# Adding the input on GpSimd instead of VectorE, with the start and the edges put in another order, in a modulated convolution kernel

## What is computed

```python
def _layer(x, style, w, b, mw, mb, typ):
    s = style @ mw.T + mb
    weight = SCALE * w * s[:, None, :, None]
    demod = lax.rsqrt(jnp.sum(weight * weight, axis=(2, 3)) + EPS)
    weight = weight * demod[:, :, None, None]
    if typ == 'same':       # convolution + bias
    elif typ == 'upsample': # transposed convolution of stride 2 + bias, then blur (1,3,3,1)
    elif typ == 'downsample': # blur (1,3,3,1), then convolution of stride 2 + bias
for i, typ in enumerate(('same', 'upsample', 'same', 'downsample')):
    out = _layer(out, style, weights[i], biases[i], mod_w[i], mod_b[i], typ)
x = x + out
```

## Time and profile before

| | |
|---|---|
| median of 3 runs | 175.73 us (174.91 to 176.23) |
| profiled execution | 177.4 us, span 175.6 us |
| TensorE busy | 162.1 us, 92% of the span, 4015 records |
| VectorE busy | 136.0 us, 77% |
| GpSimd busy | 84.0 us, 48% |
| ScalarE busy | 56.0 us, 32% |
| mean granted clock of TensorE | 0.987 |
| transfers | 17.81 MB, mean 101 GB/s |

### The profile page before, as it was taken

How to read it: one execution, slowest core, us unless ns; L and a number is a source line. 1 busy time by engine, 2 the same in 40 slices (tenths; PEclk the granted TensorE clock), 3 DMA queues, 4 the chain that set the end, 5 groups by cost and what they waited for, 6 DMA issues and landing times. The chain is left out here.

```text
span 175.6 us, 8950 instructions
## 1 busy us (share of the span) xinstructions
PE 162.1 (92%) x4015; PEld 147.4 (84%) x4015; DVE 136.0 (77%) x239; ACT 56.0 (32%) x126; POOL 84.0 (48%) x138
## 2 busy tenths in 40 slices
PE   7999879979998899999899999999999999999960
PEld 5688766969767589899798999989899999999940
DVE  7639972789599598979496878787879797979992
ACT  3244533405113133333323233424242424231110
POOL 7009905218064081939173646464647473748400
PEclk9999978999999999999999999999999999999998
DMA  4970000030300301249082633333333343030332
GB/s 127 344 116 0 6 0 4 4 119 7 119 4 6 119 6 30 97 192 292 5 279 89 235 127 123 123 123 123 123 123 123 123 123 123 4 122 5 122 127 120
DMA packets 9382, 17.81 MB, mean 101 GB/s; under 512 B 4704, under 2 KB 5248, under 8 KB 9344
## 3 DMA queue, kind: packets, MB, share of 16 engines
q1 hardware_dynamic: 9280, 17.22, 28.7%
q10 hardware_dynamic: 64, 0.02, 0.1%
HBM read 8.85 MB, written 8.39 MB: 98 GB/s over the span
## 5 line engine op out<-in xcount | busy, mean ns | idle before, releaser
L187 POOL TENSOR_TENSOR Hw<-Hw 128x192 f32<-128x192 f32 x15 | 9.0, 600 | 67.3 <-DVE Hw L791 67.3
L458 PE MATMUL p_m<-uu,Hw 64*64 64x128 f32 x992 | 31.7, 268 | 0.0
L378 PE MATMUL p_lo<-xin,w0s 64*64 64x259 f32 x384 | 28.3, 407 | 1.9 <-DVE e_sb L817 1.9
L458 PEld LDWEIGHTS p_m<-uu,Hw 64*64 64x64 f32 x992 | 29.6, 132 | 0.0
L423 PE MATMUL p_le<-R_sb,F_st 64*64 64x128 f32 (+2 forms) x768 | 27.2, 275 | 1.2 <-issue 1.1
L378 PE MATMUL p_le<-xin,w0s 64*64 64x260 f32 x384 | 26.9, 391 | 0.0
L423 PEld LDWEIGHTS p_le<-R_sb,F_st 64*64 64x64 f32 x768 | 24.5, 139 | 1.9 <-issue 1.9
L448 PE MATMUL p_m<-u,Hw 64*64 64x256 f32 x384 | 25.8, 375 | 0.0
L802 DVE TENSOR_TENSOR uu<-u 128x516 f32<-128x516 f32 x32 | 23.8, 792 | 1.5
L654 ACT ACTIVATE u<-p_lo 128x518 f32<-128x518 f32 x16 | 9.7, 604 | 45.6 <-PE p_lo L378 45.6
L254 POOL COPY Hw<-Hw 64x896 f32<-64x896 f32 x15 | 23.6, 1575 | 0.9
(11 more groups left out here) (133 smaller groups left out, 216.5 us busy)
## 6 DMA issues: line engine op xcount, KB each, us to landing
xin<-in_x_dram SPq DMA_DIRECT2D x16, 512.0 KB, 4.3
out_dram<-ot SPq DMA_DIRECT2D x16, 512.0 KB, 3.1
wn<-in_L_cond_weights_dram SPq DMA_DIRECT2D x1, 192.0 KB, 3.3
mwn<-in_L_cond_mod_w_dram SPq DMA_DIRECT2D x1, 128.0 KB, 2.2
xe<-in_x_dram SPq DMA_DIRECT2D x2, 56.0 KB, 8.6
cn<-in_cond_dram ACTq DMA_DIRECT2D x1, 16.0 KB, 2.0
bn<-in_L_cond_mod_b_dram ACTq DMA_DIRECT2D x1, 1.0 KB
bn<-in_L_cond_biases_dram ACTq DMA_DIRECT2D x1, 1.0 KB
```

The lines of the kernel that those rows point to most:

```text
L378: ins = pe.matmul(bank[h * C:(h + 1) * C, s, 0:n], w0s[p % 2][rows, k, :], xin[p % NX][rows, i0:i0 + 2 * n - 1:2], start=(k == 0), stop=(k ...
L458: ins = pe.matmul(bank(h)[s * C:(s + 1) * C], tap(p, h, s, blk), moving(slice(h * C, (h + 1) * C), s, k), start=(k == 0), stop=(k == len(b ...
```

## The change

The changed kernel differs in these parts.

- VectorE's finish no longer writes z_sb. GpSimd adds x to s_sb and to e_sb (add_x, tiles sx), and finish writes the output tile ot straight from PSUM: the product times W_D3 plus sx, one STT for the odd and one for the even positions. For this the last demodulation has moved into s and e: t_sb is scaled by W_D3 on ScalarE, s_sb and e_sb are made in two halves each, as STT. VectorE waits for x_added_odd and x_added_even, GpSimd for s_made, e_made and z_made; put_edges(p) now waits for the finish of its pair.
- The weights are loaded twice, side by side (wn2), mod_w and wsum are copied twice, and one matmul with 128 columns stands for each two of 64 in the products of the start (`taps`, `both`). The transposes of wsum stand ahead of the style; V_st is copied by GpSimd.
- layer0_odd(1), layer0_even(1) and edge_x0 have moved from the loop into the start. In the loop edge_y, edge_z and edge_out stand at the end of TensorE's iterations 0, 1 and 2, and behind finish on VectorE.
- Loads wait for mid_done, and the three early stores have their own places in iterations 4, 6 and 8, behind m2_done.

```diff
+        wn2 = sb("wn", [C, LAYERS, 2, C, K])
+        wn = wn2[:, :, 0]
...
-        z_sb = bufs(sb, "z_sb", 2, [P, 2, 2 * NM])
-        e_sb = sb("e_sb", [P, 2, NM])
+        e_sb = bufs(sb, "e_sb", 2, [P, 2, NM])
+        sx = bufs(sb, "sx", 2, [P, 2, 2, NM])
...
+            pool.wait_ge(made["wsum"], 1)
+            pool.wait_ge(zeroed, 7)
+            V = wn[:, 2].rearrange("o i k -> o k i")
+            pool.tensor_copy(V_st[0:C], V).then_inc(copied["V_st"], 1)
+            pool.wait_ge(copied["V_st"], 1)
+            pool.tensor_copy(V_st[C:P], V).then_inc(copied["V_st"], 1)
...
             def put_edges(p):
+                pool.wait_ge(z_made, 2 * (p + 1))
...
+            def add_x(p, parity, to, signal):
+                x0 = xin[p % NX][:, 1 + EDGE + parity:1 + EDGE + parity + 1]
+                x0 = bass.AP(x0.tensor, x0.offset, [list(x0.ap[0]), [BASE, 2], [2, NM]])
+                pool.tensor_tensor(sx[p % 2][:, parity], to[:], x0, ALU.add).then_inc(signal, 1)
             for p in range(-1, PAIRS):
+                if p >= 0:
+                    pool.wait_ge(x_loaded[p % NX], 16 * (p // NX + 1))
+                    wait(pool, z_made, 2 * (p - 1))
+                    pool.wait_ge(s_made, 2 * (p + 1))
+                    add_x(p, 1, s_sb[p % 2], x_added_odd)
+                    pool.wait_ge(e_made, 2 * (p + 1))
+                    add_x(p, 0, e_sb[p % 2], x_added_even)
+                if p == LATE - 1:
+                    for q in range(LATE - 1):
+                        put_edges(q)
                 if p + 2 < PAIRS:
                     sum_blocks(pool, p + 2)
                     place_H(p + 2)
-                for q in range(LATE) if p == LATE - 1 else (p,) if p >= LATE else ():
-                    put_edges(q)
+                if p >= LATE - 1:
+                    put_edges(p)
...
+            for h in range(2):
+                sp.dma_start(wn2[:, :, h], weights.rearrange("l o i k -> o l i k")).then_inc(w_loaded[h], 16)
...
-                wait(sp, out_made, p - NX + 1)
+                wait(sp, x_added_even, p - NX + 1)
...
-                sp.wait_ge(out_made, p + 1)
+                sp.wait_ge(z_made, 2 * (p + 1))
...
+                if p in (LATE, LATE + 2, LATE + 4):
+                    sp.wait_ge(m2_done, p + 1)
+                    store(n)
+                    n += 1
...
                 if p + 4 < PAIRS:
-                    sp.wait_ge(H_done, min(p + 3, PAIRS))
+                    sp.wait_ge(mid_done, p + 1)
                     load(p + 4)
-                if LATE - 1 <= p < 2 * LATE - 2:
-                    store(2 * (p - LATE + 1))
-                    sp.wait_ge(H_done, p + 4)
-                    store(2 * (p - LATE + 1) + 1)
-                if p >= 2 * LATE - 2:
-                    store(p)
+                if p >= LATE - 1:
+                    sp.wait_ge(z_made, 2 * (p + 1))
+                    store(n)
+                    n += 1
...
-                    for h in range(2):
-                        ins = pe.matmul(bank[h * C:(h + 1) * C, c0 + k * C:c0 + (k + 1) * C],
-                                        wn[:, l, :, k], ident[0:C, 0:C], start=True, stop=True)
+                    ins = pe.matmul(bank[:, c0 + k * C:c0 + (k + 1) * C], taps(l, k), ident[0:C, 0:C],
+                                    start=True, stop=True)
...
+            layer0_odd(1)
+            compose_H(1)
...
+            ins.then_inc(put["zc"], 1)
+            edge_x0()
...
+            ins.then_inc(put["oc"], 1)
+            layer0_even(1)
...
-                if p + 1 < PAIRS:
+                if 0 < p < PAIRS - 1:
                     layer0_odd(p + 1)
                     layer0_even(p + 1)
+                if p + 2 < PAIRS:
+                    compose_R(p + 2)
...
+                if p == 0:
+                    pe.wait_ge(made["x0e"], 1)
                 if p == 1:
-                    pe.wait_ge(made["x0e"], 1)
+                    pe.wait_ge(made["ye"], 1)
...
+                product_1_mid(p)
+                product_3(p)
                 if p < 3:
-                    pe.wait_ge(s_made, p + 1)
+                    pe.wait_ge(s_made, 2 * (p + 1))
                 if p == 0:
-                    edge_x0()
+                    edge_y()
                 if p == 1:
-                    edge_y()
+                    edge_z()
                 if p == 2:
                     edge_out()
...
-            V = wn[:, 2].rearrange("o i k -> o k i")
-            copy(V_st[0:C], V)
-            copy(V_st[C:P], V, copied["V_st"])
...
-                act.activation(t_sb[p % 2][:], p_m2[:, :, 0:NQ], ACT.Identity, bias=pcol(W_C, p))\
+                wait(act, s_made, 2 * (p - 1))
+                act.activation(t_sb[p % 2][:], p_m2[:, :, 0:NQ], ACT.Identity, bias=pcol(W_C, p), scale=pcol(W_D3, p))\
...
-                wait(dve, z_made, 2 * (p - 1))
-                dve.tensor_tensor(s_sb[p % 2][:].rearrange("p h (j b) -> p h b j", b=2),
...
+                wait(dve, x_added_odd, p - 1)
+                wait(dve, e_made, 2 * (p - 1))
+                for h in range(2):
+                    dve.scalar_tensor_tensor(out=s_sb[p % 2][:, h].rearrange("p (j b) -> p b j", b=2),
+                                             in0=p_m2[:, h, NQ:3 * NQ].rearrange("p (b j) -> p b j", b=2),
+                                             scalar=pcol(W_D3, p),
+                                             in1=t_sb[p % 2][:, h].unsqueeze(1).to_broadcast([P, 2, NQ]),
+                                             op0=ALU.mult, op1=ALU.add).then_inc(s_made, 1)
...
+                wait(dve, x_added_even, p - 1)
+                for h in range(2):
+                    dve.wait_ge(s_made, 2 * p + h + 1)
+                    dve.scalar_tensor_tensor(out=e_sb[p % 2][:, h].rearrange("p (j b) -> p b j", b=2),
+                                             in0=p_lo[:, h, 2 * NQ:3 * NQ].unsqueeze(1).to_broadcast([P, 2, NQ]),
+                                             scalar=pcol(W_D3, p),
+                                             in1=s_sb[p % 2][:, h].rearrange("p (j b) -> p b j", b=2),
+                                             op0=ALU.mult, op1=ALU.add).then_inc(e_made, 1)
...
-                def parity(a, part, add):
-                    dve.tensor_tensor(z_sb[p % 2][:, :, a::2], part, add[:], ALU.add).then_inc(z_made, 1)
...
+                n = NM - 1
+                def parity(a, part):
+                    o = ot[p % NO_T][:, EDGE + a:EDGE + a + 1]
+                    o = bass.AP(o.tensor, o.offset, [list(o.ap[0]), [2 * n, 2], [2, n]])
+                    y = bass.AP(part.tensor, part.offset, [list(part.ap[0]), [part.ap[1][0] + part.ap[2][0], 2],
+                                                           [part.ap[2][0], n]])
+                    add = sx[p % 2][:, a]
+                    add = bass.AP(add.tensor, add.offset, [list(add.ap[0]), [NM + 1, 2], [1, n]])
+                    dve.scalar_tensor_tensor(out=o, in0=y, scalar=pcol(W_D3, p), in1=add,
+                                             op0=ALU.mult, op1=ALU.add).then_inc(z_made, 1)
+                dve.wait_ge(m13_done, p + 1)
+                dve.wait_ge(x_added_odd, p + 1)
                 wait(dve, stored[p % NO_T], 16 * (p // NO_T))
+                parity(1, p_m13[:, :, 1])
+                dve.wait_ge(x_added_even, p + 1)
+                dve.wait_ge(m1_done, p + 1)
+                parity(0, p_le[:, :, 0:NM] if p == PAIRS - 1 else p_m13[:, :, 0])
...
-                dve.scalar_tensor_tensor(out=ot[p % NO_T][:, EDGE:L - EDGE].rearrange("p (h n) -> p h n", h=2), in0=z,
-                                         scalar=pcol(W_D3, p),
-                                         in1=xin[p % NX][:, EDGE + 1:L - EDGE + 1].rearrange("p (h n) -> p h n", h=2),
-                                         op0=ALU.mult, op1=ALU.add).then_inc(out_made, 1)
...
+            make_diffs(0)
...
+            make_uu(0)
+            demodulation(3, 4)
+            ts(vec[:, V_SB1, 0:B], style[:, 2, :], bias[:, 1:2])
+            sum_taps(0)
+            then()
+            dve.wait_ge(put["yc"], 1)
...
+            sum_blocks(dve, 0)
...
+            dve.wait_ge(put["zc"], 1)
...
+            sum_taps(1)
...
+            edge_x0()
+            dve.wait_ge(put["oc"], 1)
+            for rows, of in halves:
+                tt(pvec[rows, W_C], p_m13[rows, 1, 0, of], pvec[rows, W_D3], ALU.mult)
...
-                if p == 0:
-                    edge_x0()
-                if p == 1:
-                    edge_y()
-                if p == 2:
-                    edge_out()
                 add_mid(p)
                 if p + 2 < PAIRS:
                     sum_taps(p + 2)
                 finish(p)
-                add_x(p)
+                if p == 0:
+                    edge_y()
                 if p == 1:
                     edge_z()
+                if p == 2:
+                    edge_out()
```

264 lines of the change are left out of this document (110 added, 154 removed).

## The result

The changed kernel takes 177.78 us (median, 176.49 to 179.41) against 176.25 us (174.91 to 178.66) for the kernel before in the same comparison: a ratio of 1.0078, 95% interval 1.0053 to 1.0103. It is 0.8% slower; forecast was 166.7 us and 9 us faster. The profiled execution has a span of 175.9 us.

A forecast was written before the change was run, and what follows sets the result against it. TensorE bounds the loop at 8.58 us a period; gains lie in start, edges, stretched periods and tail. -3.9 - 4.4 - 1.4 + 0.7 = -9.0: 168.4 us profiled, 166.7 median; range 163.6 to 170.3.

The forecast's parts named there:

- Start: Before the loop: shorter demodulation chain and filled TensorE wait bring the first product to 27.0 from 30.92, minus 3.9 us.
- The gain of the new order: In the start: wsum's transposes ahead of the style and V_st on GpSimd help bring dt_ earlier; 1.2 us forecast.
- The 0.3 us for edge_x0: In the start: VectorE's five edge_x0 pieces, about 1.7 us together, end just inside TensorE's work; 0.3 us added.
- The rule: VectorE instructions with two SBUF inputs and GpSimd instructions reading SBUF shut each other out; in the loop the sum stays zero.
- The fear that TensorE's lower clock stays: In the start: lower bound, slow clock stays, gain 2.3 instead of 3.9 us; part of the half-gain rival, chance 0.23.
- Edges: First three loop periods: moving edge work to the iterations' ends cuts the excess from 8.2 to 3.7 us; minus 4.4 taken.
- Stretched periods: Three loop periods together 2.1 us over 8.6: spacing stores and load apart removes most, minus 1.4 us, bounds 0 and 2.1.
- DVE and GpSimd in the loop: Free loop periods: VectorE's reduced work and GpSimd's adds of 1.3 us each stay hidden behind 8.6 us; zero change.
- Tail: After the last pairs: finish waits for GpSimd's adds and put_edges follows, plus 0.7 us, bounds minus 0.3 and plus 1.6.
- The rivals: Whole kernel: half gain 169.7 us (0.23), better ends 164.2 (0.14), GpSimd the bound 190.5 (0.04), no effect 175 (0.05).
- the change does not do what it says: Start and loop: moved edges only shift the wait, VectorE's chain binds the start; within 1%, 175 us; chance 0.05.
- signs of being wrong: GpSimd adds over 1.9 us or no idle, start clock 0.5, TensorE waiting for z_made, periods over 9 us at transfers.

The follow-up runs named there:

- e3: Changed kernel with each product of the start issued twice at 64 columns, weights loaded once, new order kept: 172.74 us, ratio 0.9787 to the kernel before.
- e9: Kernel before with only the start's products made 128 columns wide, with the second weight load and copies: ratio 1.0113 to the kernel before.
- e14: e11 with only the first eighth of each of the first nine outputs stored: 168.98 us, ratio 0.9592 to the kernel before.
- e10: e3 with the second load of the weights, and TensorE's wait for it, kept: 172.52 us, ratio 0.9783 to the kernel before.
- e1: Changed kernel with the start up to dt_ put back and all start products at 64 columns: 173.86 us, ratio 0.986 to the kernel before.
- e5: e3 with GpSimd's sums and copies for the filter of pair 1 waiting until x0e is made: 171.16 us, ratio 0.9744 to the kernel before.
- e11: e5 with GpSimd's copies for pair 2's filter waiting for ye, and the last put_edges ahead of its adds of x: 170.21 us, ratio 0.9675.
- e6: e3 with the three early stores moved from iterations 4, 6 and 8 to 12, 13 and 14: 172.82 us.
- e2: Changed kernel with only the old order of the start put back, 128 columns kept: 177.52 us, ratio 1.0072 to the kernel before.
- e12: e3 with 128 columns for the three late products of the start alone: 175.25 us, ratio 0.9920 to the kernel before.

## Why the prediction was wrong

**Start, -3.9 forecast, +3.7 measured: the step that failed.** It stands in the sentence "The change halves the number of matmuls by giving each 128 weight columns", which counted instructions and let half as many take half the time. A wide record takes over three times as long as a narrow one at the same clock (0.14 to 0.04 us). e3 and e9 show the cost from both sides: 5.0 us back without the width in the new kernel, some 1.1% lost with it in the old. About 3.5 us of it are the records themselves, the rest is time at the lower level, and that it follows from the width is not shown.

With the width taken out, dt_ comes at 9.20 (9.15 forecast), but that is luck in part. In the trace that the prediction read, the narrow products ran at half rate, though the column reads 1.00 there: the style took 1.07 us, where e3 needs 0.66 for the same 16 records. Halving the count of slow records gave nearly the time of the full count of fast ones. The style in the kernel before, and in e14:

```profile
6.39 1.07 PE L345 MATMUL p_m<-cT,mwT 128*64 128x32 f32 x16 [0.25 <-ACT mwT L615]
```

```profile
7.11 1.07 PE L394 MATMUL p_m<-cT,mwT 128*64 128x32 f32 x16
```

In e10, where part of the narrow products run slowly again, and in e14, where all do, dt_ comes at 10.01 and 10.50. The gain of the new order was right in size, 1.1 us between e1 and e3.

**The 0.3 us for edge_x0 ahead of the first product.** VectorE's five pieces were priced from rows in which GpSimd did something else. Beside its copies they took 1.4 us more, and e5 gives 1.6 us back. The rule was cited, and then applied to uu alone. With both mistakes removed the first product stands at 27.07, 27.0 predicted: the order of the start was read rightly, though two errors of some 0.4 us cancel (the second blurred taps end at 19.8 in place of 20.2 in e11, which has the same first product, and what follows takes 7.3 us in place of 6.8; zc and edge_x0 were priced too low). The fear that TensorE's lower clock stays was right in its kind, for it lasts to 18 us; it is some 1.8 us of the loss in this trace, and the clock alone can move the first product by 1.4 us (e11 and e14, last section).

**Edges, -4.4 forecast, -3.4 measured.** The mechanism held: no wait for e_sb is left. The periods are 10.88, 10.26 and 9.44 us where 10.1, 10.1 and 9.3 stood. 0.7 of the missing 1.0 is the same contention, at ye: in e11 the first one is 10.19 and the three together 29.91 us, 4.1 under before.

**Stretched periods, -1.4 forecast, -0.8 measured** (pairs 3 to 8: 45.07 to 44.31 us). The supposed cause, two stores close to a load, fell with e6. Transfers are in it (e14), but that the new queue order is a remedy is not shown: 0.8 us is within what the same loop shows from trace to trace.

**DVE and GpSimd in the loop: zero, right.** An add on GpSimd takes 1.30 us (1.3 forecast), a half of s or e about 0.48 (0.44), a finish 0.75 (0.7), GpSimd's period 6.5 us (7.2 to 7.7, too high, as its copies fell to 0.93 each). A free period of the changed kernel; z_made comes 3.0 us behind the start of e (3.1):

```profile
104.39 1.30 POOL L276 TENSOR_TENSOR sx<-s_sb,xin 128x512 f32<-128x512 f32 x1 [1.52 <-DVE s_sb L846]
105.13 0.88 DVE L857 SCALAR_TENSOR_TENSOR e_sb<-p_lo,pvec,s_sb 128x256 f32<-128x256 f32 x2 [0.91 <-PE p_lo L492]
...
106.08 1.30 POOL L276 TENSOR_TENSOR sx<-e_sb,xin 128x512 f32<-128x512 f32 x1 [0.39 <-DVE e_sb L857]
...
107.42 0.75 DVE L874 SCALAR_TENSOR_TENSOR ot<-p_m,pvec,sx 128x510 f32<-128x510 f32 x1 [0.25 <-POOL sx L276]
```

**Tail, +0.7: right, term by term.** product_3(15) waits 0.53 us for the finish of pair 14 (0.6), the last STT waits for GpSimd's second add, and put_edges follows it:

```profile
168.33 1.53 PE L482 MATMUL p_m<-u,Hw 64*64 64x256 f32 x24 [0.53 <-DVE ot L874]
...
171.79 0.75 DVE L874 SCALAR_TENSOR_TENSOR ot<-p_le,pvec,sx 128x510 f32<-128x510 f32 x1 [0.44 <-POOL sx L276]
172.61 0.19 POOL L261 COPY ot<-oep 128x6 f32<-128x6 f32 x1 [0.85 <-DVE ot L874]
```

**The rivals.** None had the width of the matmuls as its mechanism; the one that came nearest in its result, "the change does not do what it says", got there by other means. Of the signs of being wrong, two came: a clock of 0.5 in the start, and a period over 9 us. The bounds of the start (2.3 to 4.8) took its sign for granted, though a row of wide products stood in the prediction's own rows: zc, 128*128, takes 0.83 us for 6 records, 0.14 us each, where 16 records of 64 columns take 0.66.

## What to carry to other kernels

Before two narrow matmuls are merged into one wide one, compare the time of the two groups, not their counts: in these rows 16 narrow records took 0.66 us and the 8 wide ones in their place 1.09. When an STT with two SBUF operands stands on the path to TensorE, look at what GpSimd copies in those microseconds; a wait that moves the copies was worth 1.6 us, and a second one, with put_edges moved as well, 0.95. Where a change has several parts, price each by a row of its own kind; here a single part turned a gain of 2.1% into a loss of 0.8%.

## What the runs showed of the hardware that was not expected

- The same wide product costs more than its two halves at either clock level: for the style 1.09 against 0.66 us at the upper one, and 1.92 (e2) against 1.07 us (the kernel before) at the lower.
- Two executions with the same instructions up to 17 us left the lower level 2 us apart or more (e10 and e12). e11 and e14 issue the same up to the first product; in e14 the style takes 1.07 us instead of 0.66, and the first product comes at 28.46 instead of 27.07. A start should not be priced from one trace.
- In the kernel before, the granted clock reads 1.00 from 11 to 14 us, while layer 0 runs at half its rate there (2.84 us instead of 1.4) and some of its weight loads take 225 ns instead of 131. In e2 it reads 1.00 from 6 to 18 us, and the style takes 1.92 us for the records of 1.09; and among the twenty executions of the changed kernel those with a mean clock of 0.995 are no faster than those with 0.969 (177.69 and 177.78 us). At the very start the clock column can't be relied on; the durations can.
- TensorE can run dry inside an unbroken stream of matmuls when stores and loads run beside it: 0.2 to 1.1 us a time. Splitting the transfers into halves at other places made the kernel 2.9 us slower.
